# Transposing the gathered x of a mixture-of-experts kernel by DMA copies and VectorE's 32x32 blocks in place of TensorE

## The reference, cut to what matters

```
base = einsum('bsi,oi->bso', x, W_base)
lora = einsum(z(x), ...) * scaling            # rank 16, adapter chosen per sequence
y    = base + lora
probs = softmax(y @ gate_w.T);  topk_w, topk_idx = top_k(probs, 2);  topk_w /= sum
g, u = y @ w_gate[e].T, y @ w_up[e].T
h    = silu(g) * u
out  = x + sum over the 2 chosen experts of  topk_w * (h @ w_down[e].T)
```

## Time and profile before

| what | us |
|---|---|
| three runs | 362.22, 362.49, 362.62 (median 362.49) |
| the profiled execution, first to last instruction (span) | 360.6 |
| TensorE busy in it | 348.6 |
| VectorE, ScalarE, GpSimd busy | 198.2, 179.5, 135.5 |

### The profile page before, as it was taken

One profiled execution on the slowest core, in us unless ns is written; L12 is line 12 of the kernel. 1 busy time (PEld: TensorE's weight loads), 2 busy tenths in 40 slices (PEclk: granted clock), 3 DMA queues, 4 the chain that ended last, 5 costly groups with the idle time before them and its releaser, 6 DMA issues.

```text
span 360.6 us, 7506 instructions
## 1 busy us (share of the span) xinstructions
PE 348.6 (97%) x2007; PEld 309.4 (86%) x2007; DVE 198.2 (55%) x275; ACT 179.5 (50%) x242; POOL 135.5 (38%) x85
## 2 busy tenths in 40 slices
PE   8999999999999999999999999999999999999990
PEld 4777878789899999999999999999999998898970
DVE  0486799985638264544565536556282556556210
ACT  1588611524474554444764466464545457564320
POOL 0000000113634364655745437546264456532131
PEclk9999999999999999999999999999999999999996
DMA  8993865648497948678598684976929475920322
GB/s 296 391 450 118 320 239 186 234 143 307 149 362 225 276 87 262 155 219 229 121 291 263 188 257 77 297 211 184 334 42 307 106 222 159 304 42 7 55 34 37
DMA packets 28913, 73.78 MB, mean 205 GB/s; under 512 B 3440, under 2 KB 3568, under 8 KB 28784
## 3 DMA queue, kind: packets, MB, share of 16 engines
q1 hardware_dynamic: 19904, 54.30, 42.6%
q0 software_dynamic: 8960, 18.89, 23.8%
HBM read 60.59 MB, written 19.92 MB: 223 GB/s over the span
## 4 chain that ended last, share of the span: by engine, by line
PE 91%; DMA 3%; DVE 3%; issue 1%; POOLq 0%; ACT 0%; POOL 0%; DVEq 0%
PE bank L653 41%; PE bank L682 22%; PE bank L585 5%; PE bank L410 4%; PE bank L627 4%; PE bank L510 4%; PE bank L511 3%; PE bank L514 3%; DMA xg<-y_rows,gidx 2%; PE bank L426 1%; PE bank L441 1%; PE bank L537 1%; DMA y_rows<-y_st 1%; POOLq L92 0%; PE bank L571 0%
## 5 line engine op out<-in xcount | busy, mean ns | idle before, releaser
L1185 POOL DMA_INDIRECT out<-ys,sidx x40 | 81.2, 2030 | 123.4 <-ACT ys L813 57.3
L1164 POOL DMA_INDIRECT xg<-y_rows,gidx x40 | 53.8, 1345 | 95.5 <-issue 80.5
L348 DVE TENSOR_TENSOR w_lo<-w_raw,w_hi (+2 forms) x32 | 76.3, 2385 | 21.5 <-ACT w_hi L346 16.0
L653 PE MATMUL bank<-w_hi,xt_hi 128*128 x320 | 82.2, 333 | 0.2 <-issue 0.2
L653 PE MATMUL bank<-w_hi,xt_lo 128*128 x320 | 78.7, 322 | 0.0
L653 PE MATMUL bank<-w_lo,xt_hi 128*128 x320 | 78.6, 322 | 0.0
L346 ACT ACTIVATE w_hi<-w_raw (+2 forms) x32 | 64.8, 2024 | 9.4 <-issue 6.2
L653 PEld LDWEIGHTS bank<-w_hi,xt_lo 128*128 128x128 f32 x320 | 56.0, 188 | 0.0
L653 PEld LDWEIGHTS bank<-w_lo,xt_hi 128*128 128x128 f32 x320 | 56.0, 188 | 0.0
L804 ACT ACTIVATE sg<-bank 128x352 f32<-128x352 f32 x40 | 18.5, 463 | 74.5 <-PE bank L653 74.5
L653 PEld LDWEIGHTS bank<-w_hi,xt_hi 128*128 128x128 f32 x320 | 54.2, 189 | 0.8 <-issue 0.7
(11 more groups left out here) (178 smaller groups left out, 368.2 us busy)
## 6 DMA issues: line engine op xcount, KB each, us to landing
w_raw<-wall SPq DMA_DIRECT2D x16, 1408.0 KB, 7.5
w_raw<-wall SPq DMA_DIRECT2D x16, 768.0 KB, 10.6
x_st<-xt SPq DMA_DIRECT2D x8, 512.0 KB, 12.5
y_rows<-y_st SPq DMA_DIRECT2D x16, 256.0 KB, 4.0
head_sb<-head SPq DMA_DIRECT2D x2, 640.0 KB, 4.9
wb_sb<-wb SPq DMA_DIRECT2D x2, 512.0 KB, 8.4
wbt_sb<-wbt SPq DMA_DIRECT2D x2, 512.0 KB, 10.6
xg<-y_rows,gidx POOLq DMA_INDIRECT x40, 6.1
```

Source lines behind the costliest of these rows:

```text
L348: e.tensor_tensor(w_lo[:, bass.ds(dst, n)], raw, hi, ALU.subtract).then_inc(own, 1)
L653: mm = e.matmul(bank[2 + 2 * s + t % 2][:, 0:INTER], a, w[:, bass.ds(at + (k * GU + s * INTER), INTER)], start=k == 0 and i == 0, stop=k = ...
L1164: e.indirect_dma_start(out=xg[t % NXG][:], out_offset=None, in_=y_dram, in_offset=bass.IndirectOffsetOnAxis(ap=gidx[:, t:t + 1], axis=0)). ...
L1185: e.indirect_dma_start(out=out, out_offset=bass.IndirectOffsetOnAxis(ap=sidx[:, t:t + 1], axis=0), in_=ys[t % NYS][:], in_offset=None, bou ...
```

## The change

Tiles 0 to 3 are still turned by TensorE. From tile 4 on (`N_PE`) three things replace `x_turn`:

- SP copies the gathered tile within the on-chip memory by four DMAs (`rows_apart`): copy q takes the columns q * 128 to q * 128 + 127 of all 128 rows and writes them into 32 partitions, four rows to a partition. There are three such staging tiles, `xs`.
- VectorE transposes it in blocks of 32x32 (`x_turned`) into `xt[t % 2]`, with an order of elements such that block k of x holds the features 4p + k. The gate and up weights are laid out on the host in the same order, and TensorE's four remaining x_turn read with a step of four.
- ScalarE's and VectorE's split of x read `xt` in place of bank 0.

SP's queue now holds the copies, in the order of the tiles. The weights from run 2 on are asked for by ScalarE's queue (`next_weights`), once in an iteration whose tile is the first of its run. A single semaphore counts landed gu and one landed dn, so a load is issued only once all earlier ones of its kind have landed (`landed`). A gather into a buffer of tile 4 or later waits for the four copies out of it.

```diff
+N_PE, NXS = 4, 3
+Q = 32
...
+        xs = [r_e(f"xs{i}", [P, H], F32) for i in range(NXS)]
+        xt = [r_e(f"xt{i}", [P, H], F32) for i in range(2)]
...
-        d_w = {part: [sem(f"d_{part}{i}") for i in range(NRAW)] for part in PARTS}
+        d_w = {part: sem(f"d_{part}") for part in PARTS}
+        d_xs = [sem(f"d_xs{i}") for i in range(NXS)]
+        v_xr = sem("v_xr")
...
+        def x_rows(t):
+
+            return bank[0][:] if t < N_PE else xt[t % 2][:]
+
+        def load_weights(e, ex, at, landed):
+
+            for part, (off, n) in PARTS.items():
+                if landed is not None:
+                    e.wait_ge(d_w[part], landed)
+                e.dma_start(w_raw[:, bass.ds(at + off, n)], wall[bass.ds(ex, 1), :, off:off + n].rearrange("a p n -> p (a n)"),
+                            max_dma_last_dim=ROW_GU if part == "gu" else ROW_DN).then_inc(d_w[part], 16)
...
-                        e.wait_ge(d_w[part][0], (run // 2 + 1) * 16)
-                        e.wait_ge(d_w[part][1], ((run + 1) // 2) * 16)
+                        e.wait_ge(d_w[part], (run + 1) * 16)
...
-            e.wait_ge(d_g[N_LATE], 16)
-            for r in range(2, NEXP):
-                load_weights(e, runs, r)
+                    load_weights(e, table(e, T_REX, 0, 0, NEXP - 1), EW, None)
+
+            def rows_apart(t):
+
+                n = t - N_PE
+                e.wait_ge(d_g[t % NXG], 16 * (t // NXG + 1))
+                if n >= NXS:
+                    e.wait_ge(v_xr, n - NXS + 1)
+                for q in range(P // Q):
+                    e.dma_start(xs[n % NXS][q * Q:(q + 1) * Q, :], xg[t % NXG][:, q * P:(q + 1) * P]
+                                ).then_inc(d_xs[n % NXS], 16)
...
+            with ExitStack() as rest:
+                for t in range(N_PE, NTILE):
+                    go_on(e, rest, count, t)
+                    rows_apart(t)
...
-                        mm = e.transpose(bank[0][:, k * P:(k + 1) * P], xg[t % NXG][:, k * P:(k + 1) * P], ident)
+                        rows = xg[t % NXG][:].rearrange("p (r k) -> p k r", k=KH)[:, k]
+                        mm = e.transpose(bank[0][:, k * P:(k + 1) * P], rows, ident)
...
-                    if t + 1 < NTILE:
+                    if t + 1 < N_PE:
                         x_turn(e, count, t + 1)
...
-                    e.wait_ge(m_xt, t + 1)
+                    if t < N_PE:
+                        e.wait_ge(m_xt, t + 1)
+                    else:
+                        e.wait_ge(v_xr, t - N_PE + 1)
                     if t >= 2:
                         e.wait_ge(m_gu, t - 1)
-                    e.activation(xt_hi[t % 2][:], bank[0][:], ACT.Copy).then_inc(a_xt, 1)
+                    e.activation(xt_hi[t % 2][:], x_rows(t), ACT.Copy).then_inc(a_xt, 1)
...
+            runs = table(e, T_REX, T_RUNS, TOPK, NEXP)
+
+            def next_weights(t, word):
+
+                run, new, at, _ = word
+                with e.If(new * SKIP + runs - run > SKIP + NRAW):
+                    e.wait_ge(v_dn, run + 1)
+                    load_weights(e, table(e, T_REX, bass.ds(run + NRAW, 1), 0, NEXP - 1), at, (run + NRAW) * 16)
+
+            one = ahead
...
+                        with e.If(runs > NRAW):
+                            e.wait_ge(v_dn, 1)
+                            load_weights(e, table(e, T_REX, NRAW, 0, NEXP - 1), EW, NRAW * 16)
+                        next_weights(1, one)
+                    if t < NTILE - NRAW:
+                        next_weights(t, here)
                     if t + 2 < NTILE:
                         split_weights(e, count, t + 2, ahead, "gu", a_gu)
...
-                    e.tensor_tensor(xt_lo[t % 2][:], bank[0][:], xt_hi[t % 2][:], ALU.subtract).then_inc(v_xt, 1)
+                    e.tensor_tensor(xt_lo[t % 2][:], x_rows(t), xt_hi[t % 2][:], ALU.subtract).then_inc(v_xt, 1)
+
+            def x_turned(t):
+                n = t - N_PE
+                with in_use(e, count, t):
+                    e.wait_ge(d_xs[n % NXS], (n // NXS + 1) * 16 * (P // Q))
+                    if n >= 2:
+                        e.wait_ge(v_xt, t - 1)
+                    e.transpose(xt[t % 2][:].rearrange("p (k i g) -> p g k i", k=KH, g=P // Q),
+                                xs[n % NXS][:].rearrange("p (g j k) -> p g k j", g=P // Q, k=KH)).then_inc(v_xr, 1)
...
-                        y_low(t + 1)
-                    if 3 <= t < NFULL:
-                        split_weights(e, count, t + 1, word, "gu", v_gu)
+                        with in_use(e, count, t + 1):
+                            if t >= NFULL:
+                                split_weights(e, count, t + 1, word, "gu", v_gu)
+                            y_low(t + 1)
+                            if 3 <= t < NFULL:
+                                split_weights(e, count, t + 1, word, "gu", v_gu)
                     if t < NTILE:
-                        product(t)
-                    if NFULL <= t < NTILE:
-                        h_low(t)
+                        with in_use(e, count, t):
+                            product(t)
+                            if t >= NFULL:
+                                h_low(t)
+                    if N_PE <= t + 2 < NTILE:
+                        x_turned(t + 2)
                     if t + 1 < NTILE:
                         split_weights(e, count, t + 1, word, "dn", v_dn)
...
-                    if t >= NXG:
-                        e.wait_ge(m_xt, t - NXG + 1)
+                    old = t - NXG
+                    if 0 <= old < N_PE:
+                        e.wait_ge(m_xt, old + 1)
+                    if old >= N_PE:
+                        e.wait_ge(d_xs[(old - N_PE) % NXS], ((old - N_PE) // NXS + 1) * 16 * (P // Q))
...
-    gu = np.concatenate([get[n].transpose(0, 2, 1).reshape(NEXP, KH, P, INTER) for n in ("L0_ffn_w_gate", "L0_ffn_w_up")], axis=3)
+    gu = [get[n].transpose(0, 2, 1).reshape(NEXP, P, KH, INTER) for n in ("L0_ffn_w_gate", "L0_ffn_w_up")]
+    gu = np.concatenate([g.transpose(0, 2, 1, 3) for g in gu], axis=3)
```

More of the change, by code:

```diff
@@ L88, with build @@
 R_TRI, R_ONE, R_REV, R_THR, R_CUM, R_TH3, R_IM, RW = 0, P, 2 * P, 2 * P + 16, 2 * P + 32, 2 * P + 288, 2 * P + 293, 3 * P + 293
-def build(nc, cst, rcst, head, head2, wt, wpt, wb, wbt, xt, x, wall, out):
+def build(nc, cst, rcst, head, head2, wt, wpt, wb, wbt, xin, x, wall, out):
     with ExitStack() as ctx:
@@ L273, in in_use @@
                 with eng.If(count > t):
+                    before = surely.get(eng.engine, NFULL)
+                    surely[eng.engine] = t + 1
                     yield
+                    surely[eng.engine] = before
         surely = {}
@@ L288, in table @@
         def table(eng, row, at, least, most):
-            return nc.values_load(tabs[0:1, row, at:at + 1], engines=[eng.engine], min_val=least, max_val=most,
+            cell = at if isinstance(at, bass.DynSlice) else slice(at, at + 1)
+            return nc.values_load(tabs[0:1, row, cell], engines=[eng.engine], min_val=least, max_val=most,
                                   skip_runtime_bounds_check_because="made on the chip, from counts that the shapes bound")
@@ L300, in tile_word @@
             return run, eng.snap((word // W_NEW) & 1), eng.snap(((run + 1) & 1) * EW), eng.snap((word // W_SLOT) * EW)
-        def load_weights(e, runs, r, parts=("gu", "dn")):
-            with e.If(runs > r) if r >= TOPK else nullcontext():
-                if r >= NRAW:
-                    e.wait_ge(v_dn, r - NRAW + 1)
-                ex = table(e, T_REX, r, 0, NEXP - 1)
-                for part in parts:
-                    off, n = PARTS[part]
-                    at = (r + 1) % NRAW * EW + off
-                    e.dma_start(w_raw[:, at:at + n], wall[bass.ds(ex, 1), :, off:off + n].rearrange("a p n -> p (a n)"),
-                                max_dma_last_dim=ROW_GU if part == "gu" else ROW_DN).then_inc(d_w[part][r % NRAW], 16)
+        def x_rows(t):
[6 more added lines that the diff above has]
+                            max_dma_last_dim=ROW_GU if part == "gu" else ROW_DN).then_inc(d_w[part], 16)
         def split_weights(e, count, t, word, part, own, first=0):
@@ L320, in split_weights @@
                 if act:
-                    e.wait_ge(d_w[part][0], 16)
+                    e.wait_ge(d_w[part], 16)
                     e.wait_ge(v_xlo, 2 * NBATCH)
@@ L358, in load_x @@
                 for i, half in enumerate(halves):
-                    load(x_st[b][:, half], xt[b][:, half], d_x[b][i])
+                    load(x_st[b][:, half], xin[b][:, half], d_x[b][i])
             load(head_sb[:], head, d_wt[0])
@@ L390, in _ @@
                     e.wait_ge(v_w12, 1)
-                    load_weights(e, runs, 1)
+                    load_weights(e, table(e, T_REX, 1, 0, NEXP - 1), 0, 16)
                 if c == C_LOAD:
                     e.wait_ge(v_tab, 1)
-                    runs = table(e, T_REX, T_RUNS, TOPK, NEXP)
-                    load_weights(e, runs, 0)
```

(15 more changed lines are left out.)

3 lines of the change are left out of this document (1 added, 2 removed).

## The result

The changed kernel takes 386.25 us (median of 4 runs, 385.5 to 387.8) against 362.36 for the kernel before, measured beside it: a ratio of 1.067 (95% interval 1.064 to 1.070), 24 us slower. The forecast was 366.1 with a range to 376. The direction was right, the size was not, and the time is outside the range.

What follows compares the result with a forecast made beforehand. TensorE, 97% busy, was taken to bound the kernel. The terms -15.8 + 7.7 + 6.5 + 3.2 + 2.0 gave +3.6 us: span 364.2, forecast time 366.1 us, range 351 to 376.

Steps and rivals of the forecast that it cites:

- the start: Iteration 3: ScalarE waits for run 2's weights to land before asking for run 3's; 6.5 us lost, 2.5 to 8.
- Rival 1: Requests don't hold ScalarE, since landings are early and issue is short; only the last tiles cost; 348.7 us, chance 0.25.
- rival 2: Only the issue on ScalarE is short, 0.1 us instead of 0.93; 360.8 us, chance 0.13.
- x transposes leave TensorE: Tiles 4 to 39: 36 tiles lose 0.44 us each on TensorE, 15.8 us gained.
- five two-tile runs, the stall: Iterations 14, 16, 21, 23, 31: ScalarE's request delays split, silu, product and TensorE by 1.54 us each, 7.7 us.
- iteration 33 and the tile behind it: Iteration 33: VectorE's down split ends at 304.35, then request, split, silu and product make TensorE late; 3.2 us lost.
- the last tiles: Iterations 32, 34, 36: TensorE already waits for VectorE's product, and the new transpose adds to it; 2.0 us lost.
- the way from release to split: On ScalarE in two-tile runs: 0.46 us to first DMA, 0.93 issue, 0.20 for the split's registers.
- x itself: Four 64 KB copies a tile, hidden by an 18 us lead; about 250 GB/s; cost taken as 0, upper bound 5 us.
- the gain: On TensorE, 0.44 us a tile from dropped x transposes, period 6.72 to 6.28 us; 15.8 us over 36 tiles.
- Rival 3: More is late than counted: a 1.37 us transpose adds 5.6 us, delayed landings 5; 372 to 377 us, chance 0.17.

Runs made afterwards that it cites:

- The fillers: The changed kernel with throw-away matmuls on TensorE ahead of the h transposes that are late: 376.86 us, ratio 1.043 to the kernel before.
- the trace without copies: The changed kernel with TensorE turning all tiles, no copies and no VectorE transposes, ScalarE still asking for weights: 386.39 us, ratio 1.067 to the kernel before.
- the fastest version: Changed kernel, but SP asks, a landing semaphore per raw slot, seven tiles by TensorE, VectorE turning three ahead from 25th iteration: 356.89 us, ratio 0.982 to kernel before.

## Why the prediction was right and where it was wrong

**Right: place and chain.** Requests on ScalarE hold the split, this the silu, this the product, this TensorE, in iterations 14, 16, 21, 23, 31 and 33, and nowhere in three-tile runs; one large stall at the start; a small loss in the tail. Rival 1 (the requests don't hold ScalarE) has fallen at iteration 14, and rival 2's short issue at the measured 1.00 us.

**Step by step**, in us:

| term | forecast | measured |
|---|---|---|
| x transposes leave TensorE | -15.8 | -13.0 |
| five two-tile runs, the stall | 7.7 | 11.2 |
| five two-tile runs, the tile behind it | none | 6.5 |
| the start | 6.5 | 10.8 |
| iteration 33 and the tile behind it | 3.2 | 5.7 |
| the last tiles | 2.0 | 2.4 |
| others | | 0.3 |
| sum | +3.6 | +23.8 |

**The step that failed is one that isn't there: the sum had no term for TensorE's clock.** It read the granted clock of 1.00 from a stage in which TensorE never stood, and carried it over to a kernel in which it stands for 1.8 to 5.4 us seven times. The fillers measured it at 9.4 us, nearly half of the error of 20. It was the one mechanism that was missing; the rest of the error is in the sizes of terms that were there.

**Mis-sized: the way from release to split.** It was put at 0.46 + 0.93 + 0.20, and took 0.74 + 1.00 + 0.72. The pieces, from the chain that ended last:

```profile
183.60 0.28 ACTq L299
184.22 0.40 ACTq L321
184.83 0.39 ACTq L321
185.71 0.11 ACTq L355
```

The 0.46 were SP's, with the expert's number a constant place in the table, where ScalarE reads it from a place that it has to work out (L299). The 0.20 was a guess without a row; a branch, the wait for the landing and the registers of the split stand there. The release itself came only 0.16 us later than before (2.73 against 2.57 behind the start), although VectorE's transpose took 1.138 us and not 0.69, within the bounds of 0.44 to 1.37. The stall is 2.24 us on average in place of 1.54.

**Mis-sized: the start.** The chain was right (ScalarE waits for run 2's landing before it may ask for run 3's down weights), and its silu was forecast for about 112 and came at 113.93. The landing was taken at 11.2 us, as before, and took 13.26, so it came at 110.15 and not 108.7; in the trace without copies the same landing took 11.62. From there to the split are 1.32 us in place of 0.66. And 2.2 us are the clock, in the fourth period. The copies were costed at nothing with a lead of "three tiles, 18 us", which the first tile that needs them doesn't have; here VectorE's wait for them lay inside the longer wait for the weights, and their cost was the longer landing, which the term's upper figure of 8 allowed for. The figures of "x itself" were right as means, as the stage from 100 to 290 us shows in windows of the changed kernel (columns as in the earlier trace rows, about 250 GB/s forecast); what a mean hides is the moment when weights and x are wanted together.

```profile
100.00:290.00 190.00, 174.89 (x941) 159.75 (x940) 121.13 (x126) 94.83 (x126) 89.41 (x53) 0.94 0.84 237
```

**Mis-sized: the gain.** 0.44 was read from one iteration whose pieces add to 6.72. The starts of the h transposes show 6.64 and 6.71 in turn, and after the change 6.31: 0.36 a tile.

**The rivals.** Rival 3 had the larger transpose and late landings (which came at the start alone), but as an alternative to the forecast with 5 us each; they came together with it, and with the clock. The range ended at 376 because each rival was priced alone.

**Open.** Why the clock fell behind stalls of 1.84, 1.90 and 1.98 us but not behind the one of 2.14 wasn't settled. Nor was the run-to-run spread of the fastest version (353.1 to 362.7, where the kernel before stays within 1.6 us). Its traces show stalls that move between weights and x from version to version with the DMA engines at 0.9 and more of their time, which suggests landings, but no run took that load away.

## What to carry to other kernels

A request for data is cheap on a queue that nobody waits behind and dear on an engine that has work behind it: before moving one, count the wait, the register loads and the issue, and what stands behind. A stall on TensorE is priced twice, once for its length and once for the slower clock that may follow it. And where a new stream shares the engines with an old one, look at the first moment when both are needed at once, not at the mean share.

## What the runs showed of the hardware

- VectorE's 32x32-block transpose of a 128x512 float32 tile takes 1.138 us (36 of them), against 0.686 us for a subtraction of the same shape. The Trainium skill (Vector Engine (DVE) Microarchitecture Reference, 3.8 The reshape front-end and per-opcode configuration) says that such reshapes go at one element per cycle per lane; here 512 elements a lane took 1.138 us; no run shows the length of a cycle of VectorE, so none can confirm or refute the rule, and by the rows the subtraction's time is too low a price for it by two fifths.
- After waits of 1.9 to 2.5 us in front of the h transposes the granted clock averaged 0.73 over the next 6.3 us, in three of the four windows shown; with matmuls of no use in the wait it was 1.00 in the window shown. Behind stalls of 1.38 to 1.48 us (the kernel in which TensorE turns all tiles) the granted clock was 1.00 over the next tile, behind the first four of the five.
- Two DMA issues on ScalarE take 1.00 us in iteration 14. It stands 0.74 before them, 0.28 of it for reading the expert's number, and 0.72 behind them, for a branch, a wait and the registers of the split; a wait with a tiny operation in the same place costs 0.89 from release to split.
- Copying 256 KB a tile within the chip in four parts raised the stage's traffic from 212 to 253 GB/s and the DMA engines' busy share from 0.73 to 0.92, in the version that asks behind the silu and turns seven tiles by TensorE. Its stage from 100 to 290 us, to be read beside the earlier trace rows:

```profile
100.00:290.00 190.00, 185.11 (x1048) 168.91 (x1047) 129.62 (x137) 104.48 (x140) 89.77 (x58) 1.00 0.92 253
```
